# Cross-attention and a gated layer in float32 on one core: exponentials moved ahead of a rounding, a half-width idle product, and three early loads on ScalarE's queue

## What is computed

```python
def xattn(x, context, Wq, Wk, Wv, Wout, bout):        # 8 heads of 128, batches joined
    qh = _split_heads(x @ Wq); kh = _split_heads(context @ Wk); vh = _split_heads(context @ Wv)
    sim = einsum('hid,hjd->hij', qh, kh) * 128 ** -0.5
    mean = mean(sim, axis=-1)
    attn = softmax((sim - mean) * 1.5 + mean)
    return merge_heads(einsum('hij,hjd->hid', attn, vh)) @ Wout + bout

def ffn(x, W_r, W_k, W_v, mu_r, mu_k):
    x_prev = x shifted down by one row within its batch
    xr = mu_r * x + (1 - mu_r) * x_prev;  xk = mu_k * x + (1 - mu_k) * x_prev
    return sigmoid(xr @ W_r.T) * (relu(xk @ W_k.T) ** 2 @ W_v.T)

x = x + xattn(layernorm(x), ctx_768, ...)
x = x + ffn(layernorm(x), ...)
```

## Time and profile before

| what | us |
|---|---|
| median of three runs | 737.61 |
| lowest, highest | 736.58, 738.24 |
| the profiled execution, its own time | 737.94 |
| its span | 736.1 |
| TensorE products, busy | 731.1 (99%) |
| TensorE weight loads, busy | 624.6 (85%) |
| VectorE, busy | 535.3 (73%) |
| ScalarE, busy | 422.6 (57%) |
| GpSimd, busy | 140.2 (19%) |

### The profile page before, as it was taken

How to read it: one execution, slowest core, us unless ns; L and a number is a source line. 1 busy time by engine, 2 the same in 40 slices (tenths; PEclk the granted TensorE clock), 3 DMA queues, 4 the chain that set the end, 5 groups by cost and what they waited for, 6 DMA issues and landing times.

```text
span 736.1 us, 13201 instructions
## 1 busy us (share of the span) xinstructions
PE 731.1 (99%) x3560; PEld 624.6 (85%) x3560; DVE 535.3 (73%) x1118; ACT 422.6 (57%) x1204; POOL 140.2 (19%) x320
## 2 busy tenths in 40 slices
PE   9999999999999999999999999999999999999998
PEld 8968888888888888888888888888888888888877
DVE  2689988777667767766776776777677677767665
ACT  3578875665566556556655655565565566556342
POOL 1131211222211212221121222112122211211221
PEclk9999999999999999999999999999999999999999
DMA  9975755554555555455555555555554555553412
GB/s 341 256 195 136 218 146 170 178 169 162 173 162 167 164 178 153 158 173 160 169 162 178 153 167 165 161 167 164 178 153 157 175 159 170 163 179 110 151 58 86
DMA packets 109815, 123.01 MB, mean 167 GB/s; under 512 B 12663, under 2 KB 82705, under 8 KB 109787
## 3 DMA queue, kind: packets, MB, share of 16 engines
q1 hardware_dynamic: 109492, 122.41, 54.0%
q0 software_dynamic: 256, 0.23, 0.1%
q10 hardware_dynamic: 39, 0.04, 0.0%
HBM read 66.83 MB, written 55.57 MB: 166 GB/s over the span
## 4 chain that ended last, share of the span: by engine, by line
PE 93%; DVE 3%; ACT 1%; DMA 1%; issue 1%; SPq 0%; POOL 0%; DVEq 0%; POOLq 0%
PE ffn L521 11%; PE ffn L522 11%; PE ffn L523 11%; PE scores L522 10%; PE scores L523 9%; PE scores L521 9%; PE attended L523 8%; PE attended L522 8%; PE attended L521 8%; PE scores L704 1%; PE attended L571 1%; PE attended L570 1%; PE scores L735 1%; PE ffn L735 1%; DMA x_rows<-normed 1%
## 5 line engine op out<-in xcount | busy, mean ns | idle before, releaser
L522 PE MATMUL scores<-A_lo,xT_hi 128*128 128x462 f32 x372 | 130.1, 350 | 0.0
L521 PE MATMUL scores<-A_hi,xT_hi 128*128 128x462 f32 x372 | 129.8, 349 | 0.3 <-DVE B_lo L1045 0.3
L523 PE MATMUL scores<-A_hi,xT_lo 128*128 128x462 f32 x372 | 129.8, 349 | 0.0
L523 PE MATMUL attended<-B_hi,pT_lo 128*128 128x512 f32 x288 | 112.4, 390 | 0.0
L522 PE MATMUL attended<-B_lo,pT_hi 128*128 128x512 f32 x288 | 112.3, 390 | 0.0
L521 PE MATMUL attended<-B_hi,pT_hi 128*128 128x512 f32 x288 | 112.0, 389 | 0.0
L819 ACT ACTIVATE probs<-scores,neg_max 128x154 f32<-128x154 f32 x248 | 93.6, 387 | 26.7 <-DVE neg_max L1125 26.6
L1443 POOL TENSOR_SCALAR var<-stats 128x1 f32<-128x1 f32 x64 | 12.7, 198 | 399.8 <-DVE stats L1051 399.8
L1125 DVE TENSOR_REDUCE neg_max<-scores 128x3 f32<-128x462 f32 (+1 forms) x93 | 53.4, 579 | 44.8 <-PE scores L523 44.8
L809 ACT CAST xT_hi<-xT 128x512 fp32r<-128x512 f32 x30 | 18.7, 622 | 107.3 <-DVE xT L1065 107.2
L521 PEld LDWEIGHTS scores<-A_hi,xT_hi 128*128 128x128 f32 x372 | 70.0, 188 | 7.8 <-issue 1.2
(11 more groups left out here) (183 smaller groups left out, 1579.0 us busy)
## 6 DMA issues: line engine op xcount, KB each, us to landing
prob_rows<-probs SPq DMA_DIRECT2D x32, 704.0 KB, 3.1
probs_handed<-prob_rows SPq DMA_DIRECT2D x128, 176.0 KB, 3.4
x_rows<-normed SPq DMA_DIRECT2D x61, 256.0 KB, 2.1
handed<-x_rows SPq DMA_DIRECT2D x244, 64.0 KB, 1.9
x_in<-in_x SPq DMA_DIRECT2D x32, 256.0 KB, 2.6
square_rows<-act SPq DMA_DIRECT2D x31, 256.0 KB, 2.0
act_handed<-square_rows SPq DMA_DIRECT2D x124, 64.0 KB, 1.9
out<-x SPq DMA_DIRECT2D x31, 256.0 KB, 2.3
```

Source lines behind the costliest of these rows:

```text
L521: te.matmul(psum, left[0], right[0], start=first, stop=False)
L522: te.matmul(psum, left[0], right[1], start=False, stop=False)
L523: return te.matmul(psum, left[1], right[0], start=False, stop=last)
```

## The change

It has three parts.

1. In ScalarE's program `exponentials(1, 1, 1)` stands ahead of `values_hi(FULL)` and `values_hi(0)`, where it stood behind them.
2. TensorE multiplies one more idle product, of 64 columns, behind the first five.
3. `ctx0`, `ctx1` and the second chunk of W_k are issued in this order by ScalarE, ahead of its table load. SP issues the first and the third chunk of W_k and no context. `ctx1` has a semaphore of its own, `ctx_rest_loaded`; the turning of `ctx0` waits for `ctx0` alone, that of `ctx1` for `ctx_rest_loaded`.

```diff
-        ctx_loaded = sem("ctx_loaded")
+        ctx_loaded, ctx_rest_loaded = sem("ctx_loaded"), sem("ctx_rest_loaded")
...
-            sp.dma_start(ctx0[:], ctx_rows[0:P, :]).then_inc(ctx_loaded, 16)
-            for c in range(CC):
+            for c in (0, 2):
                 sp.dma_start(wk[:, c, :], Wk[c * P:(c + 1) * P, :]).then_inc(wk_loaded[c], 16)
...
-            def keep_busy(n):
+            def keep_busy(n, width=P):
 
                 for _ in range(n):
-                    te.matmul(T[0][:, 0:P], normed[:, 0:P], normed[:, 0:P], start=True, stop=True)
+                    te.matmul(T[0][:, 0:width], normed[:, 0:P], normed[:, 0:width], start=True, stop=True)
 
             te.wait_ge(busy_ready, 1)
             keep_busy(5)
+            keep_busy(1, P // 2)
             te.wait_ge(identity_ready, 1)
-            te.wait_ge(ctx_loaded, 32)
+            te.wait_ge(ctx_loaded, 16)
             for c in range(CC):
                 te.transpose(XB[:, c * J:c * J + P], ctx0[:, c * P:(c + 1) * P], identity[:])
+            te.wait_ge(ctx_rest_loaded, 16)
...
-            nc.scalar.dma_start(ctx1[:], ctx_rows[P:J, :]).then_inc(ctx_loaded, 16)
+            nc.scalar.dma_start(ctx0[:], ctx_rows[0:P, :]).then_inc(ctx_loaded, 16)
+            nc.scalar.dma_start(ctx1[:], ctx_rows[P:J, :]).then_inc(ctx_rest_loaded, 16)
+            nc.scalar.dma_start(wk[:, 1, :], Wk[P:2 * P, :]).then_inc(wk_loaded[1], 16)
...
             exponentials(1, 1, 0)
+            exponentials(1, 1, 1)
             values_hi(FULL)
             values_hi(0)
-            exponentials(1, 1, 1)
             values_hi(1)
```

## The result

The changed kernel takes 739.02 us in the median of 15 runs (738.21 to 742.55), the kernel before 737.92 us in the same rounds (736.58 to 738.77). The medians differ by 1.1 us. The ratio of the two sets of runs is 1.002, with a 95% interval of 1.0011 to 1.0029: slower by 0.2% and clear of no change. I had forecast 737.4 and a range up to 738.6.

The account below looks back on a forecast made before the run. TensorE's products were taken as the bound, filling 731.1 of 736.1 us. From the three-run median 737.61, less 0.40 for the exponentials, plus 0.25 for the late context, 0 for the idle product: about 737.4 us, range 735.8 to 738.6.

Parts of the forecast that it names:

- Part 1, the exponentials: Values' stage: moving three exponentials ahead removes TensorE's wait for B_lo and starts scores(2) earlier, gaining 0.40 us.
- Part 2, the idle product: Ahead of the context's turning: the product costs about 0.2 us, hidden by a 0.29 us gap; taken as 0.
- my first rival: Start of the program: the idle product fills the gap and the clock rises earlier, giving 735.8 us; chance 0.25.
- Part 3, the size of the delay: Context load at the start: ctx0 shares turns with W_k's chunk, turning between -0.1 and 1.0 us later; 0.5 taken.
- The middle between two bounds: Context load: lacking a row with two large loads on two queues, 0.5 us taken between -0.1 and 1.0.
- The rule of the Trainium skill: DMA queues at the start: whole packets drained per queue, so ctx0 has no delay or ends at 4.1 us.
- The half price: TensorE's start: with the clock rising at its old moment, the 0.5 us delay costs only 0.25 us.
- if the rise moves along with the delay, 1.0: TensorE's start: upper bound on the late context's cost, 1.0 us, if the clock's rise is delayed too.
- the slower rival: Ahead of the context's turning: TensorE idles 1.2 us, deferring the clock's rise by 3.3 us; 739.4 us, chance 0.07.
- the starting point: Whole kernel: the forecast was added to 737.61 us, the median of three runs of the kernel before.

Follow-up runs that it names:

- e3: Kernel before with only the exponentials moved ahead, loads and idle products unchanged: 737.17 us against 737.44 before, ratio 0.9997.
- e1: Kernel before with the moved exponentials and the extra idle product, its loads unchanged: 736.48 us against 737.44 before, ratio 0.9989.
- e4: Kernel before with only the extra half-width idle product added: 736.62 us against 737.44 before, ratio 0.9988.
- e8: Changed kernel with ctx0 alone put back at the head of SP's queue: 736.47 us against 737.23 before, ratio 1.0001.
- e11: Kernel before with moved exponentials, extra idle product and a half-width one between the context's turnings, one later product halved: 736.59 us against 737.66, ratio 0.9993.
- e9: Changed kernel itself, run again to compare others with it on one chip: 738.72 us against 737.66 before, ratio 1.0020.
- e2: Kernel before with only the changed loads, exponentials and idle products as before: 738.82 us against 737.44 before, ratio 1.0014.
- e12: Changed kernel with 8 idle products and two half-width ahead of the turning, repeated on another chip: 737.89 us against 737.66 before, ratio 1.0010.
- e5: Changed kernel with 8 idle products and two half-width instead of 5 and one, loads as changed: 737.25 us against 737.23 before, ratio 1.0004.
- e6: Kernel before with 2 idle products instead of 5 ahead of the turning, loads unchanged: 737.91 us against 737.23 before, ratio 1.0004.
- e7: Changed kernel with W_k's first issue on SP held back until ctx0 has landed: 740.23 us against 737.23 before, ratio 1.0043.

## Why the prediction was wrong

**Part 1, the exponentials: right.** I said 0.40 us with bounds of 0.3 and 0.45; every kernel that has it but e3 shows 9.58 us for the stage, 0.34 less (e3 shows 9.73). The wait is gone from the list of waits, and ScalarE rounds chunk 4 as soon as its products are there, at 50.24 + 6 x 0.859 = 55.39. The first product of `scores(2)` came 58.69 - 57.72 - 0.86 = 0.11 us behind the last value products, where I had 0.05. By time alone e3 can't confirm the gain.

**Part 2, the idle product: taken as 0, open.** It puts the turning off by 0.1 us (3.66 in e1, 3.57 before), and it seems to have won 0.8 us in the median (e4), which is what my first rival would give: it fills the gap ahead of the turning. That rests on the medians of e1 and e4 against one set of runs of before, each with an interval that just reaches 1, and on e8 and e11, which have it too, with medians 0.8 and 1.1 below before's and intervals that include 1. It is not shown.

**Part 3, the size of the delay: the step that failed first.** I bounded it by 1.0 us, the time at which `ctx0` and one chunk of W_k, 721 KB, would be through together, and took the middle, 0.5. It was 1.67 us in the changed kernel's profile (1.40 in e9, 1.60 in e2). The stretches of the changed kernel (length, busy time of five engines, granted clock, DMA share, GB/s) are:

```profile
1.00:2.00 1.00, 0.95 (x4) 0.95 (x5) 0.00 (x0) 0.00 (x0) 0.72 (x11) 1.00 0.39 57
2.00:3.00 1.00, 1.00 (x7) 1.00 (x6) 0.00 (x0) 0.74 (x1) 0.83 (x6) 1.00 0.71 241
3.00:4.00 1.00, 0.88 (x5) 0.69 (x4) 0.00 (x0) 0.55 (x1) 0.47 (x1) 1.00 0.94 361
4.00:5.00 1.00, 0.00 (x0) 0.00 (x0) 0.00 (x0) 0.00 (x0) 0.00 (x0) 1.00 1.06 405
```

By 4.1 us 57 + 241 + 361 + 41 = 700 KB had been moved, as I had counted, but not the right ones. Turn by turn in packets, as the view of the queues shows, `ctx0` with its 128 rows is through no sooner than W_k's chunk with its 128, and two things stood beside them that I had left out: `ctx1` with 39 KB, and the third chunk of W_k, which SP's queue began as soon as the first was out. By 4.5 us about 0.64 + 0.24 = 0.88 MB had gone, where my sum had 0.72, and 3.0 + (880 - 300) / 382 = 4.5 is when the context's rows were through: 0.4 us more than my bound. The rest, 0.2 us, lies between the last rows and the turning: its first weight load came 0.5 us behind the 3.0 of my count before (3.54), and 0.7 behind the 4.5 now (5.21). Why that takes longer beside other loads the runs don't say. "The middle between two bounds" was in any case no argument: the rows of issue already said that ScalarE's load would start no sooner than SP's, which speaks for the upper end. The rule of the Trainium skill that I had put beside it ("DMA: Bandwidth & Descriptors", Queues, rings and completion order) has each engine drain a whole packet of descriptors from one queue before it turns to the other. From it I had worked out that one load's share goes wholly ahead of the other's. The trace does not show that: between 2.6 and 3.6 us the rows of both loads went in equal numbers side by side, and neither end that I had given, no delay or 4.1 us, came.

**The half price: the step that failed next.** I held that a delay costs half, since what is lost is time at the lower level. That presumed that the clock rises at its old moment. With the measured delay, the half price and the measured gain the median would be 737.92 + 0.84 - 0.34 = 738.42; measured were 739.02, and the lower end of the interval, 1.0011, is 738.7. At the full price it is 737.92 + 1.67 - 0.34 = 739.25. That speaks, though not by a wide margin, for a rise that over many runs came later too, or for early rises gone missing, as in the profiles. A single execution can still have the half price: in e9's the keys end at 7.24 + 7.71 = 14.95 us, 0.77 later than before (5.84 + 8.34 = 14.18), for a start that is 1.40 later. That it is the idle stretch which does it is the likeliest reading and not shown: with the stretch filled the same late loads cost 0.8 us less on one chip (e12 beside e9) and 1.1 less by the medians of two (0.02 above before in e5, 1.1 in the changed kernel), with intervals that overlap, and with a stretch opened (e6) the loss is not clear of none. I had named this as a bound ("if the rise moves along with the delay, 1.0") and as the mechanism of the slower rival, and gave that rival 0.07.

Neither error alone would have left the range: the right delay at half price gives 737.61 - 0.40 + 0.84 = 738.05, my delay of 0.5 in full 737.71. A part of the miss is the starting point. The three runs that I added to had a median of 737.61, the fifteen 737.92. And 737.61 - 0.15 is 737.46, which I rounded the wrong way.

**The rivals.** The slower one, "the wait for the context grows and holds the clock down", is what the runs fit best: its own price was 739.4. That the price came so close is in part luck, since it added a rise 3.3 us later (1.66) and a delay of 0.5, and the profile has a rise 2.1 us later and a delay of 1.67. The first rival had a premise that did not hold, that `ctx0` is not late; where it is not (e1, e4), the medians fall by 0.8 to 1.0 us, which would fit its mechanism. That the runs' spread of some 2 us comes from the moment of the clock's rise is in keeping with the profiles, but there is one profile for each kernel (two of the changed one), and it stays an inference.

## What to carry to other kernels

Put what the first work waits for at the head of a queue, and start no large load on another queue at the same moment: here that brought the context 1.4 to 1.7 us late, since the two queues took turns by packets and the context's were the smaller ones. Count all that the other queue holds, not only its first load, and compare landings with landings. Holding the other loads back altogether was worse still (e7, 740.2). Where TensorE's clock has not yet risen, an idle stretch ahead of the first real work may be paid twice, as the delay and as a later rise; idle products in it may give part of that back. A change there should be judged by medians of many runs, since one profile says little about the rise.

## What the runs showed of the hardware

The same load of 197 KB, issued at 0.74 us on ScalarE's queue, landed 2.5 us later with SP's loads held back (e7) and 4.4 us later with W_k's chunks beside it on the other queue (4.1 in e9, 4.3 in e2); at the head of SP's queue with W_k behind it, it took 2.8 (e8). With both queues busy they moved packets in equal numbers, 66 to 63 in a microsecond, 0.27 to 0.10 MB. The moment of the clock's rise, read from the pace of the products, differs from execution to execution: by 4.6 us in e3 and at 9.7 in the kernel before, which are the same program up to the values' stage, and at some 11.8 in the changed kernel. And where it rose early, TensorE ran ahead of the loads and waited 0.5 to 0.7 us for W_q (e3, e4, e11).
